# Column sums of the second batch: taken from TensorE, done by DMA transposes, ScalarE sums and eight small matmuls

## What is computed

```python
q1 = fake_quant(layernorm(x), x1_scale, x1_zp)      # round(v / s + z), clipped to 0..255, then (q - z) * s
q2 = fake_quant(ctx, x2_scale, x2_zp)
x = x + q1 @ q2
y = layernorm(x)
combine = weights of the best 2 of 8 experts, from softmax(y @ W_router.T)
h = einsum('nd,erd->ner', y, A_stack) * combine[..., None]
x = x + y @ W_base.T + b_base + einsum('ner,eor->no', h, B_stack) * 2.0
```

## Time and profile before

| | us |
|---|---|
| median of 3 runs | 168.58 (168.55 to 169.04) |
| the profiled execution | 168.88 |
| its span, first to last instruction | 167.1 |
| mean granted clock of TensorE | 0.997 |

### The profile page before, as it was taken

The page is one execution under the profiler, slowest core; times in us unless marked ns, Lnnn a source line. Parts: engine busy times, 40 slices in busy tenths (PEclk is TensorE's granted clock), DMA queues, the critical chain, the costliest instruction groups (busy, mean ns, idle before and its releaser), DMA issues.

```text
span 167.1 us, 2467 instructions
## 1 busy us (share of the span) xinstructions
PE 155.1 (93%) x875; PEld 80.5 (48%) x875; DVE 127.4 (76%) x283; ACT 72.6 (43%) x96; POOL 37.9 (23%) x113
## 2 busy tenths in 40 slices
PE   6858889879999999999999999999999999999990
PEld 3324335425446654644564456445644564555540
DVE  7988668999999989999889875988485828607702
ACT  3266699869999873225005300800080008003000
POOL 8204150343000433040614153125300040000000
PEclk9999999999999999999999999999999999999998
DMA  5999999991798523605430903291327002700311
GB/s 100 367 418 409 412 409 408 408 410 63 218 330 263 201 52 74 177 16 158 95 63 4 234 17 63 48 173 34 63 46 205 4 0 44 209 0 0 129 63 65
DMA packets 23677, 26.94 MB, mean 161 GB/s; under 512 B 17776, under 2 KB 18032, under 8 KB 23664
## 3 DMA queue, kind: packets, MB, share of 16 engines
q1 hardware_dynamic: 23520, 26.78, 50.8%
q10 hardware_dynamic: 144, 0.00, 0.0%
HBM read 18.38 MB, written 4.19 MB: 135 GB/s over the span
## 4 chain that ended last, share of the span: by engine, by line
PE 60%; DVE 12%; DMA 10%; ACT 9%; SPq 3%; issue 2%; POOL 2%; DVEq 0%; POOLq 0%
PE ps L889 37%; PE ps L840 10%; DMA xs<-in_x 7%; PE ps L877 6%; ACT w_hi L412 5%; DMA stage<-in_ctx_kv 3%; DVE w_lo L625 2%; SPq L208 2%; PE ps L868 2%; PE ps L870 2%; PE ps L869 2%; ACT a L366 1%; DVE a L556 1%; DVE ar_lo L619 1%; SPq L203 1%
## 5 line engine op out<-in xcount | busy, mean ns | idle before, releaser
L889 PE MATMUL ps<-w_hi,yt_hi 128*128 128x512 f16 x128 | 38.3, 380 | 0.9 <-ACT w_hi L412 0.9
L889 PE MATMUL ps<-w_hi,yt_lo 128*128 128x512 f16 x128 | 38.2, 379 | 0.0
L889 PE MATMUL ps<-w_lo,yt_hi 128*128 128x512 f16 x128 | 37.2, 379 | 0.0
L840 PE MATMUL ps<-a,a_t 128*128 128x512 f16 x128 | 30.1, 379 | 2.2 <-ACT a L366 0.9
L366 ACT ACTIVATE a<-stage,prm,inv_s 128x1024 uint8<-128x1024 f32 x16 | 19.5, 1241 | 9.5 <-DMA stage<-in_ctx_kv 9.2
L447 ACT ACTIVATE gate<-gate,ar_undo 128x1 f32<-128x1 f32 x8 | 2.4, 295 | 46.5 <-DVE gate L661 46.5
L840 PEld LDWEIGHTS ps<-a,a_t 128*128 128x128 f16 x128 | 12.2, 98 | 16.8 <-ACT a L366 1.4
L889 PEld LDWEIGHTS ps<-w_hi,yt_lo 128*128 128x128 f16 x128 | 12.5, 98 | 15.1 <-DVE yt_lo L638 0.2
L889 PEld LDWEIGHTS ps<-w_lo,yt_hi 128*128 128x128 f16 x128 | 12.5, 98 | 14.1
L889 PEld LDWEIGHTS ps<-w_hi,yt_hi 128*128 128x128 f16 x128 | 11.5, 98 | 15.0 <-issue 2.1
L293 POOL TENSOR_SCALAR root<-mvy 128x1 f32<-128x1 f32 x8 | 1.9, 234 | 57.7 <-DVE mvy L514 57.7
(11 more groups left out here) (138 smaller groups left out, 248.1 us busy)
## 6 DMA issues: line engine op xcount, KB each, us to landing
stage<-in_ctx_kv SPq DMA_DIRECT2D x16, 512.0 KB, 5.5
stage<-in_w_t SPq DMA_DIRECT2D x8, 512.0 KB, 13.0
xs<-in_x SPq DMA_DIRECT2D x7, 512.0 KB, 12.0
out_dram<-xs SPq DMA_DIRECT2D x7, 512.0 KB, 3.0
ar_raw<-in_ar_t SPq DMA_DIRECT2D x1, 544.0 KB, 13.7
xs<-in_x SPq DMA_DIRECT2D x2, 256.0 KB, 3.8
b_raw<-in_b_t SPq DMA_DIRECT2D x1, 512.0 KB, 12.5
bias_sb<-in_bias SPq DMA_DIRECT2D x1, 512.0 KB, 13.3
```

The lines of the kernel that those rows point to most:

```text
L840: last = nc.tensor.matmul(ps[:, s1_bank(t) + h, :], a1_t[:, t % 4, k, :], a2[:, k, h * H:(h + 1) * H], start=k == 0, stop=k == K - 1)
L889: ins = nc.tensor.matmul(ps[:, OUT_BANK[p] + h, :], part, rhs[:, k, h * H:(h + 1) * H], start=k == 0 and i == 0, stop=stop and i == 2)
```

## The change

For batch 1 the 16 column-sum matmuls are taken out. SyncE transposes each of the eight quantised blocks of `a2` by DMA into the first half of the `stage` buffer that it came from: six before the transpose of tile 2's `y_hi`, one between `y_hi` and `y_lo`, one behind `y_lo`. In the transposed blocks a column of `ctx` lies along a partition, so ScalarE sums 128 columns with one accumulating copy over the eight blocks: eight `sum_columns`, which write the eight columns of `col_sum`. All wait for all eight transposes. A matmul with a column of `col_sum`, repeated 128 times, as weights and the identity as moving operand puts 128 sums into every partition: eight of these, in two groups of four, in steps 1 and 4 of tile 2's wide products, into bank 3. ScalarE scales each group into its half of `corr` (`make_later_corr`). Its order around tile 2 is written out anew: five sums, `gate_weight(2)`, a sum, the scalings of tile 3, the first half of the correction, two sums, `split_hct(2)`, the second half, `sum_row(2)`. The late product no longer waits for the correction. Batch 0 is left as it was (`make_first_corr` is the old `make_corr(0)`).

```diff
+        col_sum = sb("col_sum", [P, K], F32)
...
+        def turned_ctx(k):
+            return stage[:, k, 0:H].bitcast(F16).rearrange("p (j r) -> p j r", j=K)
...
+        SPREAD_BANK = 3
...
+            def turn_ctx(n):
+                sp.wait_ge(ctx_ready, n + 1)
+                sp.dma_start_transpose(turned_ctx(n - K), a2[:, n - K, :]).then_inc(ctx_turned, 16)
+
             for n in range(K, N):
                 load_ctx(n)
+            for n in range(K, K + 6):
+                turn_ctx(n)
             transpose_y_hi(2)
+            turn_ctx(K + 6)
             transpose_y_lo(2)
+            turn_ctx(K + 7)
             transpose_a1(4)
             store(0)
...
-            def make_corr(b):
-                act.wait_ge(colsum_done, b + 1)
-                nc.scalar.activation(corr[:, b, :].rearrange("p (h n) -> p h n", h=NH),
+            def make_later_corr(h):
+                act.wait_ge(columns_spread, h + 1)
+                nc.scalar.activation(corr[:, 1, h * H:(h + 1) * H], ps[:, SPREAD_BANK, :], ACT.Identity,
+                                     bias=col_bias, scale=col_scale).then_inc(corr_ready, 1)
...
+            def sum_columns(j):
+                act.wait_ge(ctx_turned, 16 * K)
+                act.wait_ge(rows_summed, 2)
+                if j > 1:
+                    act.wait_ge(columns_summed, j - 1)
+                turned = stage[:, :, 0:H].bitcast(F16).rearrange("p k (j r) -> p k j r", j=K)
+                nc.scalar.activation(junk[:, j % 2, :].rearrange("p (k r) -> p k r", k=K), turned[:, :, j, :],
+                                     ACT.Copy, accum_out=col_sum[:, j:j + 1]).then_inc(columns_summed, 1)
...
             split_hct(1)
-            make_corr(1)
-            for t in range(2, T):
+            for j in range(5):
+                sum_columns(j)
+            gate_weight(2)
+            sum_columns(5)
+            make_y_hi(3)
+            make_y(3)
+            make_later_corr(0)
+            sum_columns(6)
+            sum_columns(7)
+            split_hct(2)
+            make_later_corr(1)
+            sum_row(2)
+            for t in range(3, T):
                 gate_weight(t)
...
-                dve.wait_ge(corr_ready, t // TB + 1)
+                dve.wait_ge(corr_ready, 1 if t < TB else 3)
...
+            def spread_columns(h):
+                pe.wait_ge(columns_summed, 4 * h + 4)
+                if h == 1:
+                    pe.wait_ge(corr_ready, 2)
+                for i in range(4):
+                    j = 4 * h + i
+                    last = nc.tensor.matmul(ps[:, SPREAD_BANK, i * P:(i + 1) * P],
+                                            col_sum[:, j:j + 1].to_broadcast([P, P]), ident[:, :],
+                                            start=True, stop=True)
+                last.then_inc(columns_spread, 1)
...
             def late_product(t):
                 pe.wait_ge(a1t_ready, t + 1)
-                pe.wait_ge(corr_ready, 2)
                 pe.wait_ge(x1_summed, t)
...
             lora(0, stop=True)
-            for k in range(K):
-                column_sums(1, k)
-                if k == 3:
-                    transpose_hc(1)
+            transpose_hc(1)
             lora(1, stop=True)
...
                 for k in range(K):
                     wide(t, k, k == K - 1)
+                    if t == 2 and k == 1:
+                        spread_columns(0)
+                    if t == 2 and k == 4:
+                        spread_columns(1)
                     if k == 2 and t + 2 < T:
                         late_product(t + 2)
```

More of the change, by code:

```diff
@@ L179, in xattn_ffn @@
         yt_hi_in, yt_lo_in = [sem(f"yt_hi_in{i}") for i in range(2)], [sem(f"yt_lo_in{i}") for i in range(2)]
-        a1t_in = sem("a1t_in")
+        a1t_in, ctx_turned = sem("a1t_in"), sem("ctx_turned")
+        columns_summed, columns_spread = sem("columns_summed"), sem("columns_spread")
         ar_done = sem("ar_done")
@@ L367, in quantise_ctx, with make_first_corr @@
                                      bias=prm[:, 3:4], scale=inv_s[:, 2:3]).then_inc(ctx_ready, 1)
-            def make_corr(b):
-                act.wait_ge(colsum_done, b + 1)
-                nc.scalar.activation(corr[:, b, :].rearrange("p (h n) -> p h n", h=NH),
+            def make_later_corr(h):
+                act.wait_ge(columns_spread, h + 1)
+                nc.scalar.activation(corr[:, 1, h * H:(h + 1) * H], ps[:, SPREAD_BANK, :], ACT.Identity,
+                                     bias=col_bias, scale=col_scale).then_inc(corr_ready, 1)
+            def make_first_corr():
+                act.wait_ge(colsum_done, 1)
+                nc.scalar.activation(corr[:, 0, :].rearrange("p (h n) -> p h n", h=NH),
                                      ps[:, COLSUM_BANK:COLSUM_BANK + NH, :], ACT.Identity,
                                      bias=col_bias, scale=col_scale).then_inc(corr_ready, 1)
+            def sum_columns(j):
[6 more added lines that the diff above has]
+                                     ACT.Copy, accum_out=col_sum[:, j:j + 1]).then_inc(columns_summed, 1)
             def sum_row(t):
@@ L380, in sum_row @@
                     act.wait_ge(rows_summed, t - 1)
+                    act.wait_ge(columns_summed, K)
                 nc.scalar.activation(junk[:, t % 2, :], a1[:, t, :], ACT.Copy, bias=-OFFSET - MIDDLE,
@@ L461, in _ @@
             act.wait_ge(consts_ready, 2)
-            make_corr(0)
+            make_first_corr()
             peak_of_first_w()
```

## The result

The changed kernel took **172.02 us** (median of four runs, 171.37 to 172.42) against 168.69 us for the kernel before in its four runs: a ratio of 1.0203, interval [1.0181, 1.0226], +3.3 us. The forecast was 171.6 us, 3.0 us up; the measured median is 0.4 us above it and inside the range.

A forecast was written before the change was run, and what follows sets the result against it. Until 67.87 TensorE's column sums fill a wait for VectorE; after it TensorE's queue bounds the kernel. Removal 0, stall 1.0 and spreads 2.0 give +3.0 us on 168.58: 171.6 us, range 170.0 to 173.8.

The forecast's parts named there:

- stall of 1.0 us: TensorE reaches tile 2's first spreads at 73.39 and waits for ScalarE's fourth sum until 74.4: 1.0 us.
- The removal's effect on the start, 0: Without the column sums, tile 1's LoRA matmuls still begin at 67.87, waiting for VectorE's `hct_lo`: worth 0.
- rival 2: TensorE's clock falls in the gap before 67.87; 2.3 us replaces the 1.0 stall: 172.9 us, chance 0.20.
- In SyncE's own time that costs next to nothing: Eight transposes at 1.23 us issue each fit SyncE's queue; the first six end at 60.4, the eighth at 65.4.
- The queue of transfers: Ten transposes of 1.25 us back up behind ctx loads from 56.75; the eighth ctx block lands at 69.75.
- rival 1: Transfers keep up with the issue, the last landing at 67.3; TensorE never stands: 170.6 us, chance 0.22.
- rival 3: Late end of the bounds: transposes land at 71.7, TensorE stands 2.9 us: 173.5 us, chance 0.08.
- The spreads, 2.0 us: Eight fp32 spread matmuls inside tile 2's wide products add 0.25 us each to TensorE's queue: 2.0.
- No second stall: The eighth sum ends at 82.1, before TensorE asks for it at 82.8 for the second group of spreads.
- VectorE 3.0 late: The gate's exponential of tile 2 slips to 75.5, making VectorE 3.0 us late; `hct_lo` of tile 2 comes at 84.1.
- Nothing later absorbs it: After 67.87 each microsecond added to TensorE's queue is a microsecond of the result.
- rival 4: Not slower: VectorE splits tile 1 before tile 0's bias, LoRA matmuls start 1.46 earlier: 168.2 us, chance 0.04.

The follow-up runs named there:

- e4: Kernel before without the 16 column-sum matmuls of batch 1 and nothing in their place: 171.2 us, ratio 1.0134.
- e2: Changed kernel with ScalarE's sums reading the untransposed blocks and not waiting for the transposes, which are still made: 172.15 us, ratio 1.0198.
- e1: Changed kernel with the 16 column-sum matmuls of batch 1 put back where they stood, result unused: 171.76 us, ratio 1.0181.
- e6: Kernel before with the eight ctx transposes added on SyncE where the change has them, only the kernel's end waiting for them: 169.56 us, ratio 1.0068.
- e3: Changed kernel with sums that don't wait for the transposes and the 16 column-sum matmuls put back, unused: 170.58 us, ratio 1.0113.
- e5: Kernel before with eight fp32 matmuls of the spreads' shape added in tile 2's wide products, waiting for nothing, result unused: 170.44 us, ratio 1.0113.
- e9: Kernel before with VectorE's split of tile 1 ahead of tile 0's bias and tile 2's ahead of the late product's sum: 167.95 us, ratio 0.9969.
- e8: Kernel before with VectorE's split of tile 1 ahead of tile 0's bias and batch 1's 16 column-sum matmuls left out: 168.75 us, ratio 1.0023.

## Why the prediction was right, and which terms were not

The time came out as forecast, 172.02 us against 171.6, and the reading that TensorE's queue after 67.87 is the result held. The way there was in part another, and to that extent the closeness is luck. The sum was 0 + 1.0 + 2.0; its middle term, a stall of 1.0 us on a TensorE at full clock, is not in the trace of the changed kernel. In its place stand 1.6 us of half clock and 0.15 us of wait. The steps one by one:

- **The removal's effect on the start, 0: right.** The LoRA matmuls of tile 1 still wait for `hct_lo`, in the change and in e4. That the removal costs nothing else was wrong: alone it costs 2.4 us (e4), by the clock. The prediction had this as rival 2 at 0.20, with a price of 2.3 us from the kernel's start; the runs show 1.6 us in the changed kernel's trace, 2.4 in e2 and 2.7 in e4. Rival 2 therefore happened; its 172.9 did not. It had TensorE at the first spread at 75.7; in the trace that is near 74.5, as half clock lasted 3.4 us there.
- **The stall of 1.0 us: right in kind, too small, and hidden.** With the clock held (e1) the first spread starts at 74.78, 0.38 later than the forecast's 74.4, and TensorE reaches it at 73.19, 0.20 before the forecast's 73.39: together 1.6 instead of 1.0. In the change itself the half clock takes up nearly all of it, so the sign that the prediction named (1 us idle before the first spread) is missing from the trace, and the sign of an error (a clock under 1 after 66) is there. The total fits because the larger of the two delays counts, and they are nearly equal.
- **"In SyncE's own time that costs next to nothing": wrong.** I took 1.23 us for each issue from a transpose that was issued with no loads ahead of it; behind loads in flight one took 3.34, and the six 10.2 instead of 7.4. The eighth was issued at 66.89 instead of 64.2. **The queue of transfers: not seen either.** The forecast let ten transfers of 1.25 us back up from 56.75 on; all but the first two landed 3.3 to 3.4 us after their issue, so it was the late issue that set the landing at 70.3, and the forecast's 69.75 came near it by another way. The faster sums (one each 1.04 us, not 1.14) nearly made up for the rest: the fourth was done at 74.57, forecast 74.4. By themselves the eight transposes cost 0.96 us (e6).
- **The transfers keep up (rival 1): in kind, in time no.** From the third transpose on only the issue counted, as this rival had it, but with the issue 2.7 us later its landing at 67.3 became 70.3. The time it gave, 170.6, is what e3 shows when both delays are taken away. **The late end of the bounds (rival 3): no.** It had the landing at 71.7 and a stall of 2.9.
- **The spreads, 2.0 us: right.** 1.90 in the trace, 1.84 in e5.
- **No second stall: right.** The eighth sum is done at 81.84 (forecast 82.1), the second group starts at 83.06 with no wait. **VectorE 3.0 late: right.** The gate's exponential is at 75.52 (forecast 75.5), `hct_lo` of tile 2 at 84.14 (84.1), ahead of the LoRA matmuls at 85.06 (85.3); VectorE then waits 1.59 us for the late row sum, and TensorE is no later for it.
- **Nothing later absorbs it: right up to TensorE's last matmul.** It is 3.12 us late at tile 2 and 3.12 at the last LoRA matmuls. Behind them the traces differ by 0.6 us in the changed kernel's favour, which the prediction did not have.
- **Not slower (rival 4): no.** Its lever, VectorE's order, is real but small: 0.5 to 0.8 us, and only when two tiles are reordered (e9). The change itself with VectorE reordered was not run.

## What to carry to other kernels

Matmuls that fill a wait of TensorE can be worth more than nothing: before such work is taken out, look at how long TensorE then stands still, and price the stretch behind it at half clock too. A time that comes out as forecast doesn't show that the way to it was right: look in the trace for the signs that were named beforehand. When two delays end at the same place, take away each alone and then both; here each alone gave nothing back, both gave 1.4 us. And price an issue on a DMA queue from a row with the same transfers in flight ahead of it, not from a quiet stretch.

## What the runs showed of the hardware that was not expected

- TensorE's granted clock fell to half where the prediction held a fall for unlikely, because one transpose of 0.33 us stands in the gap. In e4 it fell after idle stretches of 1.77 and 2.10 us around that transpose; with the column sums in the gap (idle 0.37 us at its end) it did not (e1). It stayed at half for 3.4 us in the traces of the changed kernel and of e8, and for 6.8 us in those of e2 and e4, with TensorE fully busy for most of it. What decides the length is open. In e8 it fell at 65.5, 0.3 us into a last idle stretch of only 0.69 us; in three of e8's twelve executions it did not fall.
- A transpose issued behind loads in flight held the issuing queue: 3.34 us in the changed kernel, 3.56 in e6, instead of 1.3. That the loads are the cause was not tested by itself.
- An fp32 matmul of 128 columns runs as two instructions and costs 0.22 to 0.25 us of TensorE's queue, against 0.14 for an fp32 transpose of that size (eight in 1.09 us).
